# A graph network with layer norm on one core: transposes moved ahead of the next scores, mixing behind them, scores spread over three PSUM banks

## The chip, the cores and the metric

The kernel runs on one core of one Trainium2 chip. The metric is device time in microseconds (us) from launch to end; lower is better. Before the change it is 384.06 us, the median of three runs (383.94 to 384.15).

## The reference, cut to what matters

128 graphs of 64 nodes, 384 features each, and a 64 x 64 matrix of edge types (0 or 1 in this data) for each graph:

```
hi = h @ W1[:384] + emb[adj] @ W1[384:] + b1
hj = h @ W2[:384] + emb[adj] @ W2[384:] + b2
relevance[i, j] = sum over features of hi[i, j] * hj[i, j]
A    = softmax over j of where(adj != 0, relevance, -1e9)
h2   = relu((A @ h) @ gcn_w + gcn_b) @ Wo + bo
out  = layernorm(x + h2)
```

## The kernel before, in words

The weights are folded at the start, so that for two nodes joined by an edge the relevance is a bilinear form of x: a projection of x by one 384 x 384 matrix M, and a product with x. A group is 512 rows: 8 graphs, held as four "pairs" of 128 rows. There are 16 groups (0 to 15); `run` emits bodies 0 and 1, a hardware loop of two bodies for groups 2 to 13, then bodies 14 and 15 (`LAST` is 15). Products of large matrices run in fp32r with each operand split in a high and a low part, so each is three matmuls (L422, L423, L424 for projection and value, L515, L516, L521 for the output). Scores, transposes and mixing are plain fp32; a plain fp32 matmul shows as two records, a transpose as one.

TensorE carries for each group these stages, by function:

- `proj` (L426): 27 matmuls of 512 columns, K-block by K-block into three banks; ScalarE copies each finished bank with a bias to `gt_sb` (`project_out`, L714), and counts `gt_ready`.
- `score_stage` (L439): 24 fp32 matmuls, 128 rows x 64 columns of array, in bank 0, one graph of a column half at a time with its three blocks of K in a row. It begins with a wait for all three `gt_sb` blocks.
- VectorE then masks (`rel`, L921, four instructions, then L925 and L927), ScalarE exponentiates (`weigh`, L773), VectorE divides (L939, L941: `weights`, semaphore `normed`).
- `value` (L450): 36 matmuls, four banks (1 to 4), x times gcn_w; VectorE copies each to `hg_sb` (L825).
- `turn` (L478): two 128-column transposes of `weights` into bank 0; ScalarE copies them to `at_sb` (L795).
- `mix` (L485): 48 fp32 matmuls on 64 x 64 tiles of the array, in banks 4 to 7; ScalarE applies relu twice for each of three blocks (`hidden`, L781 and L783, counted by `hshi`), and VectorE makes the low part (`low_half`, L912, counted by `hslo`).
- `out` (L575): 36 matmuls into banks 5, 6, 7 and 1; VectorE adds x (L834, counted by `added`), takes statistics (L839) and normalises (L856), with GpSimd computing the inverse deviation (L1116).

The order on TensorE is written by hand, and each engine runs its own list in order; semaphores tie them. In a steady body g TensorE issues: mix(g-1), scores(g), value(g+1), out(g-1), turn(g), proj(g+1). Body 0 has no mix and no out, and its scores follow the second half of value(0). The last body issues mix(14), scores(15), the second half of out(13), half of out(14), turn(15), out(14) pair 2, mix(15), out(14) pair 3, and `out_last` follows. ScalarE's body g is: hidden(g-1), weigh(g), the high part of x two groups on (L708), `row_terms` of the next group (L723, the per-row term that L921 needs, semaphore `srow_ready`), the copy of the transposes (L795), `project_out(g+1)`. In the last body ScalarE runs hidden(14), weigh(15), the copy, hidden(15). SyncE loads x, its transpose and the edge matrix two groups ahead and stores results; the transposed x waits for `score_mm`, and the edge matrix for `masked`.

The first product of out(14) carries a condition of its own (L588):

```
if static(g, LAST - 1) and q == 0:
    pe.wait_ge(hshi, C * LAST if c == 0 else C * g + c + 1)
```

With C = 3 that asks for all three high blocks of group 14 (45 counts) before its first matmul.

Of the kernel before, what the change touches and what calls it, by code (L numbers as in the profile page):

```python
# [46 lines left out]
P = 128  # L47
# [5 lines left out]
def gnn_layernorm_kernel(nc, x, x_t, adj, adj_t, edge, biases, w1_t, w2_t, gcn_w, wo_w, wo_b, out):  # L53
    HID, TOKENS = x_t.shape
    NODES = adj.shape[2]
# [23 lines left out]
    with ExitStack() as ctx:  # L79
# [86 lines left out]
        score = bank[0]  # L166
        M_BANK = bank[5:8]
# [251 lines left out]
        def _(pe):  # L419
# [19 lines left out]
            def score_stage(g, par):  # L439
                pe.wait_ge(gt_ready, C * (g + 1))  # L440
                for n in range(PAIRS):
                    for c in range(C):
                        for e in range(2):
                            q, h = HALVES * e + n // 2, n % 2
                            ts = slice(q * P + h * NODES, q * P + (h + 1) * NODES)
                            mm = pe.matmul(score[e * NODES:(e + 1) * NODES, n * NODES:(n + 1) * NODES],  # L446
                                           gt_sb[:, c, ts], xt_sb[:, par, c, ts], start=(c == 0), stop=(c == C - 1))
                mm.then_inc(score_mm, 1)

            def value(g, par, q):  # L450

                if static(g, 0):
                    if q == 0:
                        pe.wait_ge(xt0_lo, 1)
                    elif q == 2:
                        pe.wait_ge(xlo, 1)
                elif q == 0:
                    pe.wait_ge(xlo, g + 1)
                    if static(g, 1):
                        pe.wait_ge(hg_ready, PAIRS)  # L460
                    elif not static(g, 2):
                        pe.wait_ge(added, PAIRS * (g - 2))
                elif q == 3 and not static(g, 1):
                    pe.wait_ge(hshi, C * (g - 1))
                ts = slice(q * P, (q + 1) * P)
                for c in range(C):
                    if static(g, 0) and q == 0:
                        pe.wait_ge(gcn_lo_ready, C + c + 1)
                    mm = three(VALUE_BANK[q][:, 0:HW], xt_hi[:, par, c, ts], xt_lo[:, par, c, ts],
                               gcn_hi[:, c, :], gcn_lo[:, c, :], c == 0, c == C - 1)  # L470
                mm.then_inc(value_mm, 1)
# [6 lines left out]
            def turn(g):  # L478
                pe.wait_ge(normed, 2 * (g + 1))
                for v in range(HALVES):  # L480
                    mm = pe.transpose(score[:, v * P:(v + 1) * P],  # L481
                                      weights[:, 2 * v:2 * v + 2, :].rearrange("p h n -> p (h n)"), ident[:])
                mm.then_inc(turn_mm, 1)
# [91 lines left out]
            def out(g, qs):  # L575

                for q in qs:
                    if q == 0 and not static(g, LAST - 1):
                        pe.wait_ge(hslo, C * (g + 1))
                    if static(g, LAST - 2) and q == 2:  # L580
                        pe.wait_ge(hg_ready, PAIRS * LAST + 1)
# [29 lines left out]
            def body(g, par):  # L611
                if not static(g, 0):
                    mix(g - 1, 1 - par)
                score_stage(g, par)
# [10 lines left out]
                if static(g, 0):  # L625
                    pe.wait_ge(ident_ready, 1)
                else:
# [3 lines left out]
                turn(g)  # L631
# [67 lines left out]
        def _(act):  # L699
# [85 lines left out]

            def body(g, par):
                if not static(g, 0):
                    hidden(g - 1)
# [5 lines left out]
                act.wait_ge(turn_mm, g + 1)  # L794
                act.copy(at_sb[:], score[:, 0:MIX]).then_inc(at_ready, 1)  # L795
                if before(g, LAST):
                    project_out(g + 1, PROJ1_BANK if static(g, 0) else PROJ_BANK)
                else:
                    hidden(g)
# [22 lines left out]
        def _(dve):  # L822
# [92 lines left out]
            def body(g, par):  # L915
# [4 lines left out]
                for q in range(PAIRS):  # L920
                    a = dve.scalar_tensor_tensor(rel[:, q, :], score[:, q * NODES:(q + 1) * NODES],  # L921
# [291 lines left out]
```

## Time and profile before

| | us |
|---|---|
| median of three runs | 384.06 |
| the profiled execution's own time | 387.24 |
| its span, first to last instruction | 385.4 |
| TensorE matmul busy | 376.2 (98%) |
| VectorE busy | 214.7 (56%) |
| ScalarE busy | 170.9 (44%) |
| GpSimd busy | 150.2 (39%) |

Matmuls are pipelined and the ends of their records are modelled, so the length of a matmul record is not its share of the time: the distance from one start to the next is. A busy share of 98% says that there is always a matmul under way, not that the array is full. A weight load (PEld) that starts together with the matmul of the same line had nothing to hide behind.

### The profile page before, as it was taken

To read this page: it belongs to the slowest core of one execution; us is meant where nothing else is said; L and a number is where in the kernel's file an instruction comes from. 1 tells how busy PE (TensorE), PEld (TensorE's weight loads), DVE (VectorE), ACT (ScalarE), POOL (GpSimd) and SP (SyncE) were. 2 spreads that over 40 slices of the span, in tenths; PEclk is the share of its full clock that TensorE was granted. 3 is DMA by queue.
4 is the path that set the end of the run, shared out by engine and by line. 5 is a ranking of instruction groups with operands and counts; after the bars stand their busy time and mean duration, and the time that the engine had idled before them with its cause. 6 is when DMAs were issued, how large, how long until landed. Compare 5 with 4: busy or idle time off the path is not lost.

```text
span 385.4 us, 10043 instructions
## 1 busy us (share of the span) xinstructions
PE 376.2 (98%) x3977; PEld 343.7 (89%) x3977; DVE 214.7 (56%) x528; ACT 170.9 (44%) x389; POOL 150.2 (39%) x133
## 2 busy tenths in 40 slices
PE   8999999999999999999999999999999999999992
PEld 4689898998989899898989989898998989898991
DVE  1535166563637656363755636375564637555684
ACT  1533561626336162633617263361726346153563
POOL 0031635080723508072350807245080724517043
PEclk9999999999999999999999999999999999999998
DMA  7922021707143170715317071531707153260105
GB/s 224 317 102 82 17 83 26 236 0 205 57 140 120 18 241 0 207 51 140 119 26 233 0 212 46 145 113 27 231 0 218 41 151 107 34 229 6 38 21 189
DMA packets 34820, 42.89 MB, mean 111 GB/s; under 512 B 10096, under 2 KB 29040, under 8 KB 34800
## 3 DMA queue, kind: packets, MB, share of 16 engines
q1 hardware_dynamic: 34144, 41.92, 36.1%
q10 hardware_dynamic: 656, 0.70, 0.7%
q8 instruction: 13, 0.21, 0.2%
q14 instruction: 7, 0.06, 0.1%
HBM read 30.03 MB, written 12.58 MB: 111 GB/s over the span
## 4 chain that ended last, share of the span: by engine, by line
PE 97%; DVE 2%; issue 0%; POOL 0%; DVEq 0%
PE banks L422 18%; PE banks L424 17%; PE banks L423 17%; PE banks L515 9%; PE banks L521 9%; PE banks L516 9%; PE banks L501 6%; PE banks L446 6%; PE banks L548 2%; PE banks L529 1%; PE banks L481 1%; DVE stats L839 1%; DVE xt_sb L834 0%; PE banks L556 0%; PE banks L540 0%
## 5 line engine op out<-in xcount | busy, mean ns | idle before, releaser
L1105 POOL TENSOR_TENSOR x_sb<-x_sb,wob_sb 128x1536 f32<-128x1536 f32 x15 | 52.5, 3503 | 177.7 <-DVE weights L941 177.7
L422 PE MATMUL banks<-gcn_hi,xt_hi 128*128 128x386 f32 x192 | 66.7, 347 | 0.0
L424 PE MATMUL banks<-gcn_hi,xt_lo 128*128 128x386 f32 x192 | 65.0, 339 | 0.0
L423 PE MATMUL banks<-gcn_lo,xt_hi 128*128 128x386 f32 x192 | 65.0, 338 | 0.0
L714 ACT ACTIVATE gt_sb<-banks,r_sb 128x512 f32<-128x512 f32 x48 | 33.0, 687 | 71.0 <-PE banks L424 70.9
L921 DVE SCALAR_TENSOR_TENSOR rel<-banks,srow,adj_sb 128x64 f32<-128x64 f32 x64 | 13.7, 278 | 85.5 <-PE banks L446 84.1
L515 PE MATMUL banks<-wo_hi,hs_hi 128*128 128x384 f32 x180 | 61.0, 339 | 0.0
L516 PE MATMUL banks<-wo_lo,hs_hi 128*128 128x384 f32 x180 | 60.9, 339 | 0.0
L521 PE MATMUL banks<-wo_hi,hs_lo 128*128 128x384 f32 x180 | 60.6, 339 | 0.0
L422 PE MATMUL banks<-xt_hi,m_hi 128*128 128x512 f32 x144 | 57.5, 399 | 0.0
L424 PE MATMUL banks<-xt_hi,m_lo 128*128 128x512 f32 x144 | 56.8, 394 | 0.0
L423 PE MATMUL banks<-xt_lo,m_hi 128*128 128x512 f32 x144 | 56.4, 392 | 0.0
L1096 POOL TENSOR_TENSOR xt_lo<-xt_sb,xt_hi 128x1536 fp32r<-128x1536 f32 x15 | 52.6, 3507 | 5.1 <-ACT xt_hi L708 5.1
L834 DVE TENSOR_TENSOR y_sb<-banks,x_sb 128x384 f32<-128x384 f32 x60 | 33.3, 556 | 29.9 <-PE banks L521 29.9
L825 DVE COPY hg_sb<-banks 128x385 f32<-128x385 f32 x64 | 35.6, 556 | 22.9 <-PE banks L424 22.8
L781 ACT ACTIVATE hs_sb<-banks,bias_sb 128x512 f32<-128x512 f32 x48 | 33.3, 695 | 16.3 <-PE banks L501 16.3
L422 PEld LDWEIGHTS banks<-gcn_hi,xt_hi 128*128 128x128 f32 x192 | 36.2, 188 | 1.1
L423 PEld LDWEIGHTS banks<-gcn_lo,xt_hi 128*128 128x128 f32 x192 | 36.4, 190 | 0.0
L424 PEld LDWEIGHTS banks<-gcn_hi,xt_lo 128*128 128x128 f32 x192 | 36.3, 189 | 0.0
L795 ACT COPY at_sb<-banks 128x256 f32<-128x256 f32 x16 | 6.0, 373 | 66.9 <-PE banks L481 66.8
L839 DVE BATCH_NORM_STATS2 stats<-y_sb 128x6 f32<-128x384 f32 x60 | 33.6, 560 | 2.0
L515 PEld LDWEIGHTS banks<-wo_hi,hs_hi 128*128 128x128 f32 x180 | 33.8, 188 | 0.1
(89 smaller groups left out, 585.0 us busy)
## 6 DMA issues: line engine op xcount, KB each, us to landing
xt_sb<-in_x_t_dram SPq DMA_DIRECT2D x15, 768.0 KB, 4.6
x_sb<-in_x_dram SPq DMA_DIRECT2D x15, 768.0 KB, 5.4
out_dram<-y_sb SPq DMA_DIRECT2D x30, 384.0 KB, 5.8
adj_sb<-in_adj_dram SPq DMA_DIRECT2D x32, 64.0 KB, 2.3
xt_sb<-in_x_t_dram SPq DMA_DIRECT2D x2, 384.0 KB, 8.4
xt_sb<-in_x_dram SPq DMA_DIRECT2D x1, 768.0 KB, 6.2
out_dram<-xt_sb SPq DMA_DIRECT2D x4, 192.0 KB, 2.0
w1t_sb<-in_w_t_dram ACTq DMA_DIRECT2D x3, 192.0 KB, 6.3
```

The lines of the kernel that those rows point to most:

```text
L422: pe.matmul(acc, a_hi, b_hi, start=first, stop=False)
L423: pe.matmul(acc, a_hi, b_lo, start=False, stop=False)
L424: return pe.matmul(acc, a_lo, b_hi, start=False, stop=last)
L515: pe.matmul(acc, hs_home(g)[0][:, c, ts], wo_hi[:, c, :], start=(c == 0), stop=False)
L516: pe.matmul(acc, hs_home(g)[0][:, c, ts], wo_lo[:, c, :], start=False, stop=False)
L521: mm = pe.matmul(out_bank(g, q)[:, 0:HID], hs_home(g)[1][:, c, ts], wo_hi[:, c, :], start=False, stop=(c == C - 1))
L781: act.activation(by_graph(hs_sb[:, f, :]), mixed(f), ACT.Relu, bias=gb_sb[:, f:f + 1]).then_inc(hsr, 1)
L825: dve.tensor_copy(hg_sb[:, slot, q, :], VALUE_BANK[q][:, 0:HID + 1]).then_inc(hg_ready, 1)
L834: dve.tensor_tensor(y_home(g, slot)[:, q, :], out_bank(g, q)[:, 0:HID], x_home(g, slot)[:, q, :], ALU.add).then_inc(added, 1)
L839: dve.bn_stats(stats[:, q, :], y_home(g, slot)[:, q, :]).then_inc(statd, 1)
L1096: pool.tensor_tensor(xt_lo[:, slot], xt_sb[:, slot], f32(xt_hi[:, slot]), ALU.subtract).then_inc(xlo, 1)
L1105: pool.tensor_tensor(x_home(g, slot), x_home(g, slot), wob_sb[:].rearrange("p (o n) -> p o n", o=1).to_broadcast([P, PAIRS, HID]), ALU.add ...
```

## The change

Transposes leave their place between out and proj. In a body g above 0 TensorE now begins with turn(g-1), then scores(g), then mix(g-1), then value(g+1), out(g-1), proj(g+1). The transposes write bank 5. The scores of graph n = 0, 1, 2 go to banks 0, 1, 2 and those of n = 3 to bank 0; for the first three graphs the first two blocks of K are done ahead of the third, and the wait for the third block of `gt_sb` stands between. Since banks 1 and 2 are also value's, value's first matmul waits for the masks of the body's scores to be read (`masked`), and so does out(13) pair 2 in the last body. The scores wait for all additions of out(g-2), and the transposes for bank 5 to be free. On ScalarE the copy of the transposes stands at the top of the next body, ahead of `hidden`. The wait for the identity matrix moves with the first transposes. Group 15's own transposes stay where they were.

```
+        SCORE_BANK = bank[0], bank[1], bank[2], bank[0]
+        TURN_BANK = bank[5]
...
             def score_stage(g, par):
-                pe.wait_ge(gt_ready, C * (g + 1))
-                for n in range(PAIRS):
-                    for c in range(C):
+                def graphs(n, blocks):
+
+                    for c in blocks:
                         for e in range(2):
                             q, h = HALVES * e + n // 2, n % 2
                             ts = slice(q * P + h * NODES, q * P + (h + 1) * NODES)
-                            mm = pe.matmul(score[e * NODES:(e + 1) * NODES, n * NODES:(n + 1) * NODES],
+                            mm = pe.matmul(SCORE_BANK[n][e * NODES:(e + 1) * NODES, n * NODES:(n + 1) * NODES],
                                            gt_sb[:, c, ts], xt_sb[:, par, c, ts], start=(c == 0), stop=(c == C - 1))
-                mm.then_inc(score_mm, 1)
+                    return mm
+
+                if static(g, LAST):
+                    pe.wait_ge(added, PAIRS * (g - 2))
+                elif not (static(g, 0) or static(g, 1)):
+                    pe.wait_ge(added, PAIRS * (g - 1))
+                pe.wait_ge(gt_ready, C * g + 2)
+                for n in range(PAIRS - 1):
+                    graphs(n, (0, 1))
+                pe.wait_ge(gt_ready, C * (g + 1))
+                for n in range(PAIRS - 1):
+                    graphs(n, (2,))
+                graphs(PAIRS - 1, range(C)).then_inc(score_mm, 1)
 
             def value(g, par, q):
...
                 elif q == 0:
+                    pe.wait_ge(masked, 3 * g - 2)
                     pe.wait_ge(xlo, g + 1)
...
             def turn(g):
                 pe.wait_ge(normed, 2 * (g + 1))
+                if static(g, 0):
+                    pe.wait_ge(gt_ready, C + 1)
+                elif static(g, LAST):
+                    pe.wait_ge(hshi, C * g)
+                else:
+                    pe.wait_ge(added, PAIRS * (g - 1) + 1)
                 for v in range(HALVES):
-                    mm = pe.transpose(score[:, v * P:(v + 1) * P],
+                    mm = pe.transpose(TURN_BANK[:, v * P:(v + 1) * P],
...
                     if static(g, LAST - 2) and q == 2:
+                        pe.wait_ge(masked, 3 * LAST + 1)
                         pe.wait_ge(hg_ready, PAIRS * LAST + 1)
...
             def body(g, par):
+                if static(g, 1):
+                    pe.wait_ge(ident_ready, 1)
+                if not static(g, 0):
+                    turn(g - 1)
+                score_stage(g, par)
                 if not static(g, 0):
                     mix(g - 1, 1 - par)
-                score_stage(g, par)
...
-                if static(g, 0):
-                    pe.wait_ge(ident_ready, 1)
-                else:
+                if not static(g, 0):
                     if static(g, 1):
                         pe.wait_ge(wo_lo_ready, 1)
                     out(g - 1, range(2 if static(g, LAST - 1) else PAIRS))
-                turn(g)
                 proj(g + 1, 1 - par, PROJ1_BANK if static(g, 0) else PROJ_BANK)
...
+            def turned_out(g):
+
+                act.wait_ge(turn_mm, g + 1)
+                act.copy(at_sb[:], TURN_BANK[:, 0:MIX]).then_inc(at_ready, 1)
+
             def body(g, par):
                 if not static(g, 0):
+                    turned_out(g - 1)
                     hidden(g - 1)
                 weigh(g)
...
-                act.wait_ge(turn_mm, g + 1)
-                act.copy(at_sb[:], score[:, 0:MIX]).then_inc(at_ready, 1)
                 if before(g, LAST):
                     project_out(g + 1, PROJ1_BANK if static(g, 0) else PROJ_BANK)
                 else:
+                    turned_out(g)
                     hidden(g)
...
-                    a = dve.scalar_tensor_tensor(rel[:, q, :], score[:, q * NODES:(q + 1) * NODES],
+                    a = dve.scalar_tensor_tensor(rel[:, q, :], SCORE_BANK[q][:, q * NODES:(q + 1) * NODES],
```

## Rows read from the trace of the kernel before

**Rows 1.** The page: busy time by engine, and the chain that ended last.

```profile
PE 376.2 (98%) x3977; PEld 343.7 (89%) x3977; DVE 214.7 (56%) x528; ACT 170.9 (44%) x389; POOL 150.2 (39%) x133
PE 97%; DVE 2%; issue 0%; POOL 0%; DVEq 0%
```

**Rows 2.** Waits: engine, tile, line, waited for; total us, times, longest us.

```profile
PE banks L529 <- DVE attn L860: 1.3, 1, 1.3
...
PEld banks L501 <- issue: 5.7, 16, 0.4
...
POOL x_sb L1105 <- DVE weights L941: 177.7, 15, 14.0
```

**Rows 3.** Timeline, steady body, around the transposes: start, us, engine, line, operation.

```profile
173.56 0.34 PE L521 MATMUL banks<-wo_hi,hs_lo 128*128 128x384 f32 x1
173.56 0.31 PEld L481 LDWEIGHTS banks<-ident,weights 128*128 128x128 f32 x2
173.74 0.38 PE L481 MATMUL banks<-ident,weights 128*128 128x128 f32 x2
173.84 0.19 PEld L422 LDWEIGHTS banks<-xt_hi,m_hi 128*128 128x128 f32 x1
...
174.19 0.39 PE L423 MATMUL banks<-xt_lo,m_hi 128*128 128x512 f32 x1
174.41 0.40 PE L424 MATMUL banks<-xt_hi,m_lo 128*128 128x512 f32 x1
```

**Rows 4.** Timeline, same body, TensorE from projection over mixing and scores to value.

```profile
179.92 0.40 PE L424 MATMUL banks<-xt_hi,m_lo 128*128 128x512 f32 x1
180.24 1.49 PEld L501 LDWEIGHTS banks<-at_sb,hg_sb 64*64 64x64 f32 x96 [0.36 <-issue]
...
181.80 1.48 PEld L446 LDWEIGHTS banks<-xt_sb,gt_sb 128*64 128x64 f32 x48
...
183.35 0.19 PEld L422 LDWEIGHTS banks<-gcn_hi,xt_hi 128*128 128x128 f32 x1
...
183.63 0.34 PE L423 MATMUL banks<-gcn_lo,xt_hi 128*128 128x386 f32 x1
```

**Rows 5.** Timeline, same body, ScalarE and VectorE.

```profile
174.15 0.37 ACT L795 COPY at_sb<-banks 128x256 f32<-128x256 f32 x1 [4.76 <-PE banks L481]
...
180.35 0.69 ACT L714 ACTIVATE gt_sb<-banks,r_sb 128x512 f32<-128x512 f32 x1 [1.38 <-PE banks L424]
...
181.94 0.69 ACT L781 ACTIVATE hs_sb<-banks,bias_sb 128x512 f32<-128x512 f32 x1 [0.90 <-PE banks L501]
...
183.47 0.86 DVE L921 SCALAR_TENSOR_TENSOR rel<-banks,srow,adj_sb 128x64 f32<-128x64 f32 x4 [5.55 <-PE banks L446]
```

**Rows 6.** Timeline, last body: VectorE's end of a block, and TensorE's release by it.

```profile
373.27 0.69 DVE L912 TENSOR_TENSOR hs_lo<-hs_sb,hs_hi 128x512 fp32r<-128x512 f32 x1
...
374.02 0.30 PEld L521 LDWEIGHTS banks<-wo_hi,hs_lo 128*128 128x128 f32 x2 [0.15 <-DVE hs_lo L912]
```

**Rows 7.** Timeline, body 0: scores, row terms, first value matmul, masks.

```profile
31.17 1.48 PEld L446 LDWEIGHTS banks<-xt_sb,gt_sb 128*64 128x64 f32 x48 [0.24 <-issue]
...
31.87 1.21 ACT L723 ACTIVATE srow<-hg_sb,k_sb 64x2 f32<-64x2 f32 x4 [3.08 <-DVE hg_sb L825]
32.72 0.45 PE L422 MATMUL banks<-gcn_hi,xt_hi 128*128 128x386 f32 x1
...
33.22 0.86 DVE L921 SCALAR_TENSOR_TENSOR rel<-banks,srow,adj_sb 128x64 f32<-128x64 f32 x4 [1.39 <-ACT srow L723]
```

**Rows 8.** Timeline, last body: hidden(14) on ScalarE, out(13) and out(14) on TensorE.

```profile
358.18 0.69 ACT L781 ACTIVATE hs_sb<-banks,bias_sb 128x512 f32<-128x512 f32 x1 [0.90 <-PE banks L501]
...
359.59 0.44 PE L515 MATMUL banks<-wo_hi,hs_hi 128*128 128x384 f32 x1
...
361.04 0.72 ACT L783 ACTIVATE xt_hi<-banks,bias_sb 128x512 fp32r<-128x512 f32 x1
...
362.87 0.33 PE L515 MATMUL banks<-wo_hi,xt_hi 128*128 128x384 f32 x1
```

## The prediction

> **What bounds the kernel now.** I read the page first. TensorE is busy 98% of the span and is 97% of the chain that ended last [rows 1], so an edit moves the time only if it lengthens or shortens TensorE's own sequence. The list of waits comes next: TensorE's longest is 1.3 us, at the very start, and no steady stage waits for another engine. What is left are small holes that the list calls "issue", 5.7 us over the 16 mixing stages, 0.36 each [rows 2]. Then the timeline of one steady body, read by distances between starts. In the projection a 512-column matmul starts 0.22 to 0.23 after the one before it (174.19 to 174.41) [rows 3]; an output matmul takes 0.18, since the transposes start 0.18 after the last of them (173.56 to 173.74) [rows 3], more exactly 0.176 (18 of them from 359.59 + 0.10 to 362.87) [rows 8]; value's, two columns longer, take the same.
>
> So the present cost of the transposes is: they start at 173.74, and the projection's second matmul at 174.19, of which 0.23 are its first one. 174.19 - 0.23 - 173.74 = 0.22 us per group. The mixing stage begins 0.32 after the start of the last projection matmul, which streams for 0.23: a hole of 0.09. Mixing takes 1.56 (180.24 to 181.80), the scores 1.55 (181.80 to 183.35), and value's first weights are loaded in the open: its second matmul starts 0.28 after the load instead of 0.18, 0.10 lost [rows 4].
>
> **The change, part by part.** Let S be the start of the last projection matmul (179.92 in the steady body), and all times below counted from it.
>
> *Transposes.* Leaving their place gives 0.22. In the new place the first follows the projection at 0.23, with its weights loaded behind it as they are behind the output matmul now [rows 3]. The second comes 0.10 later (its successor's load starts 0.10 after 173.74), at about 0.33, and streams some 0.05. Then comes a stage on another shape of tile. If it opens with the same hole as mixing does now (0.09 to 0.10), the scores' first load is at 0.49; mixing's was at 0.32. The two transposes cost 0.16 in the new place, and the move gains 0.22 - 0.16 = 0.06. The bounds: 0.03 (the hole is counted from the end of the longer fp32 record) and 0.15 (no hole at all after a transpose). Fifteen of the sixteen move (group 15's don't): 15 x 0.06 = -0.9 us, from -0.5 to -2.3.
>
> *The order of mixing and scores.* Both are small fp32 matmuls on two shapes of tile. Before, three changes of shape per body (projection to mixing, mixing to scores, scores to value); after, three again. I put the swap at 0.
>
> Why the hole should stay: mixing and scores are both fp32, and still the value stage shows its exposed load and mixing its hole at a change of shape [rows 4], while the output matmuls (fp32r, full array) pass to the transposes (fp32, full array) with none [rows 3]. The Trainium skill, "TensorEngine Tiling (Array Packing)", section Tiling Modes, says that a change of tiling mode, unlike a change of tile, drains the engine; by that rule the hole follows the shape of the tile and not the data type. It speaks against the hope that gathering the fp32 stages removes a transition, and the count of three before and three after stays; without it the sum would be lower by 15 x 0.09.
>
> *The wait for the third block of K.* ScalarE's copy of the third projection bank starts at 0.43 and takes 0.69 [rows 5]: ready at 1.12. TensorE sees a release about 0.06 later (VectorE ends at 373.96, the load goes at 374.02) [rows 6]: 1.18. The stage has 12 of its 24 matmuls to do before, 12 x 0.06 = 0.7 from 0.49: the load of the 13th is due at about 1.18. Before, mixing hid this copy; now it is met to the hundredth. I take 0 to 0.03 per group and carry +0.2 us over 15; the bound above is 0.1 each, +1.5, if the queue, empty by then, is slow to fill. In body 0 value's second half lies between, so nothing.
>
> *The wait for the copied transposes.* ScalarE takes it after the projection copy, at about 1.12, 0.37 long [rows 5]: ready by 1.55. Mixing is due at 0.49 + 1.55 = 2.04. Hidden behind the scores; without them it would cost 1.2 per group.
>
> *The new wait of value for the masks.* In a steady body VectorE begins L921 0.12 after the scores end (183.47 against 183.35) and needs 0.86 [rows 5], having been idle 5.55 before. From 2.04: masks read at 3.0, seen at 3.1; mixing lasts until 3.60. Hidden, with 0.5 to spare. Queued behind this wait are value, out and proj, everything, so where the cover is missing it is paid in full. It is missing in **body 0**, which has no mixing. There value starts at 32.72, but L921 starts only at 33.22, held by the row terms on ScalarE (31.87 + 1.21), and ends at 34.08 [rows 7]; released at 34.13. TensorE stands from 32.72 to 34.13: **+1.4 us**, and nothing after it has slack to absorb this.
>
> *Mixing 1.7 us later: what waits for it.* ScalarE's hidden starts 0.14 after mixing ends, so at 3.74 instead of 2.02 [rows 4, 5]. It takes 3.58 (358.18 to 361.76) [rows 8]: done at 7.32. In a steady body its first users are value's fourth bank, at 3.60 + 0.10 + 27 x 0.176 = 8.45, and out, at 10.1 with the low parts done by 8.1. Both hidden. GpSimd starts after the softmax, later by under 1.8, and waits 14 us at most for it, 177.7 in 15 waits [rows 2]. The loads of the transposed x and of the edges are issued earlier, since scores and masks are; SyncE has no new wait. In the **last body** the cover is thin: between mixing and out(14) lie only 18 matmuls. Before, hidden(14) ended at 361.76 and out(14) started at 362.87 [rows 8]. After: out(13) from 3.60 + 0.10 lasts 18 x 0.176 = 3.17, so the first load of out(14) is due at 6.70; it asks for all of hidden(14), seen at 7.38, and its load is then in the open. The matmul starts at 7.48 instead of 6.88: **+0.6 us** (0.4 to 0.8, as ScalarE's copies stretch). Pair 2 of out(13) waits for the masks as value does, and finds them read at 3.1. Group 15's softmax follows hidden(14) and is done about 9.3, its transposes are due at 10.6: covered. From there to the end the order is as before.
>
> **Sum.** -0.9 + 0.2 + 1.4 + 0.6 = +1.3 us; without the 0.2, +1.1. The profiled execution took 387.24 (span 385.4, 1.8 around it), 3.2 more than the median of 384.06, so a difference read from it is scaled by 0.99, which changes nothing. I predict **385.3 us**, own range 384.6 to 386.0.
>
> **The rivals.**
> 1. *The holes cost less or the move gains more, and the two stalls are cancelled.* If the transposes leave no hole the gain is 2.3 instead of 0.9: 384.06 - 2.3 + 2.0 = 383.8, within 0.2% of before (0.77 us, about what a measurement can tell). For: nothing shows a transpose ahead of a small tile. Against: rows 4.
> 2. *TensorE's supply fails between the small matmuls.* The stage of 24 scores now has a stop in it, and behind it follow mixing's several waits, with small matmuls that start every 0.016 us (96 in 1.56) [rows 4]. Now these waits are passed under long matmuls. If each of the two places (13th score, value after mixing) shows 0.05 to 0.1, 15 bodies add 1.5 to 3: 386.6 to 388.2. It decides if the stop lasts beyond 1.18 or the gap ahead of mixing grows over 0.1. For: the queue is empty at the stop. Against: before, one wait stood between mixing and scores, and the stretch is 1.56 like mixing alone.
> 3. *Faster.* The scores in three banks run quicker: today each of 24 matmuls takes 0.06; if those that now follow a matmul on another bank (9 of 24) took half, 9 x 0.03 x 16 = 4.3 us go, 381.0; it decides from 2 us on, if the scores stage falls below 1.42. For: each accumulates on what was just written. Against: mixing accumulates nothing and has the same pace per tile (96 records on four tiles, 48 on two, both in 1.56).
> 4. *The change doesn't do what it says.* If the masks' wait in body 0 were met early, 1.4 would go: 383.9. The rows leave no room for it; it is in rival 1's chance.
>
> **How the numbers follow.** Forecast 0.52, rival 1 0.20, rival 2 0.18, rival 3 0.10. The forecast's own range goes a little below 384.83 (slower by 0.2%), which moves 0.07 of it to the middle. Faster 0.10, same 0.26, slower 0.64. The range leaves out rival 3 and the upper half of rival 2: 383.7 to 387.0.
>
> **What would show it.** The list of waits has a new TensorE wait of 1.4 for L921's masks, once, and one of 0.6 at L515 for L783, once. L481 starts 0.23 after the last L424; the projection follows the output with no gap; the scores' first load is about 0.49 after the last L424; no gap within the scores; value's first load 3.6 after S. The distance from body to body falls by 0.06. Wrong would be: no wait in body 0, a steady body shorter by more than 0.15, or longer.

## The result, and the profile after

| | kernel before | kernel after |
|---|---|---|
| device time, median (lowest to highest), us | 384.11 (383.94 to 386.32), 4 runs | 390.22 (388.3 to 391.05), 4 runs |
| ratio to before, 95% interval | | 1.0127 (1.0093 to 1.0161) |
| span of the profiled execution, us | 385.4 | 388.2 |
| first score matmul to last matmul, us | 346.49 | 350.65 |

The ratio says that the change costs 1.3%, about 4.9 us (3.6 to 6.2); the two medians alone lie 6.1 apart, and I go by the ratio with its interval. 385.3 was forecast, with 387.0 as the upper end. The sign was right; the size was not.

The last line of the table is a measure that I use from here on: the distance between the starts of TensorE's first score matmul and of its last matmul, read from the trace. The whole span is a poor ruler, because the start-up varies by itself: the first scores began anywhere between 27.3 and 31.2 us in fourteen profiled executions, whatever the kernel. Behind them the work repeats to 0.01 us: three more profiled executions with the old order gave 346.48, 346.48 and 346.49.

The page of the kernel after, busy time and chain. TensorE still is the bound [rows 1], but "issue" (time in which the engine waited for nothing that the profile shows) has come into the chain with 1%, and so has ScalarE:

```profile
PE 375.1 (97%) x3977; PEld 344.5 (89%) x3977; DVE 218.1 (56%) x528; ACT 168.5 (43%) x389; POOL 150.2 (39%) x133
PE 94%; ACT 1%; DVE 1%; POOL 1%; issue 1%; DVEq 0%
```

The list of waits of the kernel after, TensorE's new entries (engine, tile, line, waited for; total us, times, longest us); it stands against [rows 2]:

```profile
PEld banks L448 <- issue: 2.8, 16, 0.2
...
PEld banks L522 <- issue: 2.4, 2, 2.1
...
PE banks L522 <- issue: 2.0, 1, 2.0
...
PE banks L424 <- DVE rel L949: 1.4, 1, 1.4
...
PEld banks L536 <- ACT xt_hi L806: 0.6, 1, 0.6
...
PE banks L536 <- ACT xt_hi L806: 0.3, 1, 0.3
```

PEld is the weight load and PE the matmul of the same stop, so two rows can tell of one. Three stops were forecast: 16 small holes, now ahead of the scores (L448) in place of mixing; once 1.4 us for the masks (VectorE's L949); and once 0.6 for hidden(14) (ScalarE's L806; 0.3 in the matmul's row). One was not: TensorE stood 2.0 us within the mixing stage (L522), once, and waited for no semaphore.

**A steady body.** Timeline of the kernel after, from the last projection matmul to mixing (start, us, engine, line, operation; in brackets the idle time before it and what ended it), against [rows 3, 4]:

```profile
157.18 0.39 PE L426 MATMUL banks<-xt_hi,m_lo 128*128 128x512 f32 x1
...
157.41 0.38 PE L502 MATMUL banks<-ident,weights 128*128 128x128 f32 x2
157.61 0.69 ACT L737 ACTIVATE gt_sb<-banks,r_sb 128x512 f32<-128x512 f32 x1 [1.37 <-PE banks L426]
157.72 1.48 PEld L448 LDWEIGHTS banks<-xt_sb,gt_sb 128*64 128x64 f32 x48 [0.17 <-issue]
...
158.20 0.36 ACT L812 COPY at_sb<-banks 128x256 f32<-128x256 f32 x1
159.27 0.27 PEld L522 LDWEIGHTS banks<-at_sb,hg_sb 64*64 64x64 f32 x12
```

The transposes start 0.23 after the last projection matmul, the scores' first load 0.31 later, at 0.54. The 48 score records run without a stop (1.55 to mixing's first load), although ScalarE's copy of the third block ends only at 158.30: the stage's second half, which needs it, is due at 158.5, so that wait is hidden, and so is the one for the copied transposes (158.56 against 159.27). A body takes 22.407 us, against 22.427 before: it gains 0.02.

**Body 0.** Timeline of the kernel after, VectorE's masks and value's first matmul, against [rows 7]:

```profile
30.80 0.46 PE L448 MATMUL banks<-xt_sb,gt_sb 128*64 128x64 f32 x10
31.70 0.86 DVE L949 SCALAR_TENSOR_TENSOR rel<-banks,srow,adj_sb 128x64 f32<-128x64 f32 x4 [1.39 <-ACT srow L746]
32.62 0.44 PE L424 MATMUL banks<-gcn_hi,xt_hi 128*128 128x386 f32 x1 [1.35 <-DVE rel L949]
```

The masks are read at 32.56 and TensorE goes on at 32.62, 0.06 later, as forecast.

**Body 14, the first one behind the loop.** Timeline of the kernel after:

```profile
338.80 1.21 PE L522 MATMUL banks<-at_sb,hg_sb 64*64 64x64 f32 x66
...
342.00 0.32 PEld L522 LDWEIGHTS banks<-at_sb,hg_sb 64*64 64x64 f32 x14 [2.12 <-issue]
342.00 0.46 PE L522 MATMUL banks<-at_sb,hg_sb 64*64 64x64 f32 x14 [1.99 <-issue]
342.38 0.19 PEld L424 LDWEIGHTS banks<-gcn_hi,xt_hi 128*128 128x128 f32 x1
```

82 of mixing's 96 matmuls are done, then nothing for 2 us, then the last 14. No engine's instruction releases them. The DMA view shows what happens there. The page of either kernel has a queue called "instruction" (q8) with 13 transfers in all; asked by windows, the first one behind the loop went at another moment. The kernel before, between 335 and 336 us (queue, kind: packets, MB, share of 16 engines):

```profile
q8 instruction: 1, 0.02, 7.2%
```

The kernel after, between 339.5 and 341 us; from 334 to 339.5 there is no such row:

```profile
q8 instruction: 1, 0.02, 3.7%
```

In the trace's record of transfers each is 16384 bytes. Before, it starts at 335.22, while TensorE still works through long projection matmuls, and mixing and scores follow at 337.2 to 340.3 without a gap. After, it starts at 339.57 and takes 0.88, to 340.45. TensorE's last matmul ahead of the pause starts at 339.80, the next one at 342.00, 1.55 behind the end of the transfer. That suggests that TensorE waited for its own code; the experiments below test it.

**The last body.** Timeline of the kernel after, against [rows 8]:

```profile
364.61 0.71 ACT L806 ACTIVATE xt_hi<-banks,bias_sb 128x512 fp32r<-128x512 f32 x1
364.72 0.33 PE L542 MATMUL banks<-wo_hi,hs_lo 128*128 128x384 f32 x1
365.38 0.45 PE L536 MATMUL banks<-wo_hi,xt_hi 128*128 128x384 f32 x1 [0.33 <-ACT xt_hi L806]
365.66 0.34 PE L537 MATMUL banks<-wo_lo,xt_hi 128*128 128x384 f32 x1
```

Matmul to matmul 0.66 instead of 0.18, and 0.28 instead of 0.18 to the one behind it, whose load is in the open: 0.6 for the 36 output matmuls (7.02 from the first to the transposes, against 6.40).

**The ledger**, from scores to scores, so that mixing, which changed its side, is counted alike (us):

| stretch | before | after | difference |
|---|---|---|---|
| scores(0) to scores(1), mixing(0) taken off before | 16.07 - 1.56 = 14.51 | 16.04 | +1.53 |
| scores(1) to scores(14), 13 bodies | 13 x 22.427 = 291.55 | 13 x 22.407 = 291.29 | -0.26 |
| scores(14) to scores(15) | 19.25 | 21.53 | +2.28 |
| scores(15) to the last matmul, mixing(14) added before | 19.61 + 1.56 = 21.17 | 21.80 | +0.63 |
| sum | | | +4.18, measured 350.65 - 346.49 = 4.16 |

So half of the loss is a thing that the prediction did not know. What may make up the rest of the 4.9 us came to light in the experiments, in the next section.

### The profile page after: what moved, and what is told of

Its sections match the earlier page's. It is cut to its first block, busy times and chain, and to the rows that moved or that the text cites. A ratio compares the mean times of both kernels' runs of the same rounds, so it can differ in the third digit from the quotient of the medians.

```text
span 388.2 us, 10086 instructions
## 1 busy us (share of the span) xinstructions
PE 375.1 (97%) x3977; PEld 344.5 (89%) x3977; DVE 218.1 (56%) x528; ACT 168.5 (43%) x389; POOL 150.2 (39%) x133
## 4 chain that ended last, share of the span: by engine, by line
PE 94%; ACT 1%; DVE 1%; POOL 1%; issue 1%; DVEq 0%
PE banks L424 18%; PE banks L425 17%; PE banks L426 17%; PE banks L536 8%; PE banks L537 8%; PE banks L542 8%; PE banks L522 7%; PE banks L448 6%; PE banks L569 2%; PE banks L550 1%; PE banks L502 1%; POOL rstd L1144 1%; ACT hs_sb L804 0%; PE banks L577 0%; ACT xt_hi L806 0%
## 5 line engine op out<-in xcount | busy, mean ns | idle before, releaser
L424 PE MATMUL banks<-xt_hi,m_hi 128*128 128x512 f32 x144 | 56.6, 393 | 0.0
L949 DVE SCALAR_TENSOR_TENSOR rel<-banks,srow,adj_sb 128x64 f32<-128x64 f32 x64 | 13.8, 277 | 61.6 <-PE banks L448 60.2
L542 PEld LDWEIGHTS banks<-wo_hi,hs_lo 128*128 128x128 f32 x180 | 33.6, 188 | 0.3
```

The costliest lines, as they stand in the source:

```text
L424: pe.matmul(acc, a_hi, b_hi, start=first, stop=False)
L542: mm = pe.matmul(out_bank(g, q)[:, 0:HID], hs_home(g)[1][:, c, ts], wo_hi[:, c, :], start=False, stop=(c == C - 1))
```

## The experiments

Each kernel was timed beside the kernel before on its chip. The kernel before had a median of 386.28 us in the first group of four, 385.69 in the second and 384.36 in the third.

**1. The kernel before once more.**

> The kernel before, unchanged. The profiled execution of it lasted 387.24 us and the median of its runs 384.06, 3.2 less; the changed kernel's profile opens with the second matmul stage (L569) 1.5 us shorter than before's (L548), because the full clock was granted 3 us earlier. If the gap of 3.2 lies in the start-up clock, a second profile of this kernel shows a span near 383.8 with L548 at 7.5 us instead of 9.0, or again 385.4 with 9.0. If there is something else that comes and goes, the spans differ while L548 is the same, and a pause on TensorE or a late load must show in one of them and not in the other.

One execution: 385.15 us, span 383.3. First scores at 28.70 instead of 31.17, and from there to the last matmul 346.48, the same as in its first profile. The 2.1 us that the span is shorter come from the start (2.5 less, and 0.3 more behind the last matmul). The windows of the first profile, from 0, 8 and 13.5 us (us, busy and instructions of PE, PEld, DVE, ACT, POOL, granted clock, DMA share, GB/s):

```profile
8.00:13.50 5.50, 5.50 (x10) 2.92 (x9) 1.64 (x3) 2.06 (x4) 0.00 (x0) 1.00 1.10 333
```

and of this execution:

```profile
8.00:13.50 5.50, 4.92 (x20) 3.01 (x19) 1.19 (x2) 1.60 (x3) 0.00 (x0) 1.00 1.07 335
```

TensorE did ten matmuls of the set-up in one and twenty in the other. This has nothing to do with the change; it is why differences are read from the first scores on. The expectation's first branch holds in the main: the stage of 18 set-up matmuls (L548) took 9.0 us in the first profile and 6.9 in this one. The trace's record of the granted clock begins, at full speed, at 13.3 us in the first and at 4.2 in this one; the 1.00 in the rows above says nothing for the time before, of which there is no record. All fourteen profiles fit this: in seven the full clock is on record from 4.2 to 6.0 us on, and the first scores start at 27.3 to 28.7; in six it is from 10.2 to 13.3 on, and they start at 29.1 to 31.2. The last one (number 7) has it from 4.4 on, but half clock again from 14.7 to 18.1, and starts at 29.7.

**2. No masked wait in body 0.** Scores(0) in one bank in the old order, and no wait ahead of value(1).

```diff
+                if static(g, 0):
+                    pe.wait_ge(gt_ready, C)
+                    for n in range(PAIRS):
+                        last = graphs(n, range(C), bank[0])
...
-                    pe.wait_ge(masked, 3 * g - 2)
+                    if not static(g, 1):
+                        pe.wait_ge(masked, 3 * g - 2)
```

> The changed kernel with the scores of group 0 alone kept in bank 0 and in the old order, so that value of group 1 needn't wait for the masks. Theory (stalls add up): TensorE's wait of 1.4 us for L949 is gone and nothing takes its place; the time is 1.4 us below the changed kernel, about 388.8, and the 2 us pause in mixing of body 14 stays. Rival (slack later absorbs it): less than 0.5 us is gained, and another wait of TensorE grows. The scores of group 0 being in one bank could also show whether three banks matter: their stage of 48 records should last the same 1.55 us.

Ratio 1.0106 (1.005 to 1.0161). Scores(0) to scores(1) fell from 16.04 to 14.61: the wait was worth 1.43, and it is gone. The whole time did not reach the 388.8 that was expected (389.98, and the interval is too wide to tell 1.4 us). The profiled execution lost some 1.5 us elsewhere. Its windows around the pause, columns as above:

```profile
338.40:341.40 3.00, 1.01 (x26) 0.81 (x18) 0.54 (x2) 0.33 (x1) 0.00 (x0) 0.99 0.98 359
341.40:344.80 3.40, 3.40 (x12) 3.40 (x12) 0.85 (x2) 3.40 (x8) 0.00 (x0) 0.51 0.11 36
344.80:350.00 5.20, 5.20 (x32) 5.20 (x31) 3.60 (x8) 1.43 (x9) 2.60 (x1) 1.00 0.00 0
```

In the first window TensorE stands for 2 us. In the second it is busy throughout, at a granted clock of 0.51, that is 1.2 GHz instead of 2.4, and starts 12 matmuls in 3.4 us; at full clock it would be some 19. Scores(14) to scores(15) took 23.07, against 21.53 in the first profile of the kernel after: 1.54 more. The pause can bring a second loss with it.

**3. The load of x(15) held back.** The DMA engines are full when the code block is fetched (share 1.03 from 337 to 340 us in the kernel after), and this load (the issue at 338.63 in the kernel after) is part of it.

```diff
+                        sp.wait_ge(mix_mm, LAST - 1)
```

> The changed kernel with one more wait on SyncE: the load of x for group 15, which now leaves at 338.63, 1.4 us into the dense matmuls of body 14, waits for mixing(13) to end. Theory A (the pause of 2.2 us in that mixing is TensorE waiting for its next 16 KB block of instructions, whose transfer at 339.7 to 340.6 stands in line behind data transfers, since all 16 DMA engines are busy from 337 on): the block comes earlier and the pause falls to under 1 us or goes; time about 388.2 to 389. Theory B (the block is asked for only when the sequencer runs into its edge, and takes 2.3 us whatever else is moving): the pause stays at 2.0 to 2.3 us and the time is that of the changed kernel, 390.

Ratio 1.0149 (1.0082 to 1.0216). The load left at 343.16, behind the pause. The pause stayed, behind the same 82nd matmul, and was 0.3 longer. Timeline of TensorE:

```profile
338.87 1.49 PE L523 MATMUL banks<-at_sb,hg_sb 64*64 64x64 f32 x82
342.62 0.45 PE L523 MATMUL banks<-at_sb,hg_sb 64*64 64x64 f32 x14 [2.26 <-issue]
```

The load of x(15) is not the cause. How much of the 2 us other transfers add was not settled; in no run were the DMA engines free at the pause (share 0.97 ahead of it here and 0.55 during it).

**4. The code shifted by 84 instructions.** Increments of a semaphore of which nobody's wait depends, spread over TensorE's bodies 0 and 1 ahead of the loop. Nothing in the order of the work changes; the code behind them stands 84 places further on.

```diff
+                for _ in range(min(2, padding[0])):
+                    pe.sem_inc(mix_begun, 1)
+                    padding[0] -= 1
...
+            padding[0] = 84
```

> The changed kernel with 84 semaphore increments that nobody waits for among TensorE's instructions of bodies 0 and 1, two ahead of every three long matmuls, where the sequencer has time. They move everything behind them by 84 places against the 256-instruction blocks in which code is fetched. Theory B (where a block ends decides): the pause in body 14 moves from the 82nd mixing record to some 42 records earlier, or goes to another stage, or is gone where the edge falls under long matmuls. Theory A (load traffic alone): the pause stays at about 340 us and at the same record, give or take. The increments themselves should cost nothing; if they do, it is seen as a longer distance from body 0 to body 2.

Ratio 1.0032 (0.9998 to 1.0065), 1.2 us over before instead of 4.9. No pause: scores(14) to scores(15) 19.23. A block was fetched at 102.4, inside the first turn of the loop, where before and after fetch none past 96.9. First scores to last matmul 348.55, 2.06 over before. The wait in body 0 grew by 0.24 (1.81 from start to start instead of 1.58) in all padded versions of the new order that have it. That is the padding's own doing: two of the idle increments stand between the wait and value's first matmul, and the trace has them at 30.64 and 30.79, behind the masks, and the matmul at 30.90.

**5. The kernel before shifted by 24**, to make it pay the pause.

```diff
+                for _ in range(min(1, padding[0])):
...
+            padding[0] = 24
```

> The kernel before with 24 idle semaphore increments in body 0's value and projection, and nothing else. Theory B (the pause belongs to where the code blocks end against the loop's exit, not to the new order): the old order now has a pause of some 2.2 us too, in the first 300 records of body 14, between 337 and 341 less the start-up difference, and the distance from the scores of group 1 to the last matmul grows from 330.4 to about 332.6. Rival (the new order's own waits starve TensorE): no pause, 330.4. The increments are hidden either way.

A miss: ratio 0.9986 (0.996 to 1.0011), no pause, a block fetched inside the loop (104.4), 346.48 from the first scores to the last matmul.

**6. The kernel after with 8 instructions fewer** (one warm-up matmul instead of three).

```diff
-WARM_UP = 3
+WARM_UP = 1
```

> The changed kernel with one warm-up matmul instead of three, which takes 8 instructions out ahead of the loop. By the places of the pauses seen so far the block edge lies some 13 instructions behind the loop's exit in the changed kernel and 16 in the one before; if so small a margin decides, 8 fewer bring the fetch back to the exit and the pause in mixing of body 14 is gone, as in the kernel before. If the pause stays, the margin is another, or the order matters too. The clock may come up at another time, so the distance from the scores of group 1 to the last matmul is what counts: 334.6 with the pause, 332.4 without.

A miss as well: ratio 1.0149 (1.0093 to 1.0204). The pause stayed (2.16 from start to start), and the half clock followed it.

**7. Shifted by 84, and the condition in front of out(14) relaxed**: its first block asks only for the first of the three parts of hidden(14).

```diff
-                            pe.wait_ge(hshi, C * LAST if c == 0 else C * g + c + 1)
+                            pe.wait_ge(hshi, C * g + c + 1)
```

> The changed kernel with the 84 increments and with the first matmul of out(14) asking for the first high block of group 14 alone (hshi 43) instead of all three. Theory (the tail's stall is the condition's): the gap of 0.66 from start to start at the first matmul of out(14) falls back to 0.18, no other gap takes its place, and the distance from the scores of group 1 to the last matmul is 0.48 less than with the increments alone. Rival (the chain is held by ScalarE's hidden all the same): a gap of 0.2 to 0.6 appears at the second or third block, or at the transposes of group 15, and under 0.2 is gained.

Ratio 1.006 (1.0024 to 1.0096); first scores to last matmul 348.23, 0.32 less than number 4. The gap of 0.66 has gone, and the three blocks of out(14)'s first pair run without a stop. One of 0.36 has come ahead of its second pair, with 0.10 behind it for a load that has nothing to hide behind. Timeline:

```profile
363.38 0.69 DVE L950 TENSOR_TENSOR xt_lo<-hs_sb,xt_hi 128x512 fp32r<-128x512 f32 x1 [0.46 <-ACT xt_hi L816]
...
364.00 0.55 DVE L872 TENSOR_TENSOR y_sb<-banks,x_sb 128x384 f32<-128x384 f32 x1
...
364.60 0.19 PEld L545 LDWEIGHTS banks<-wo_hi,xt_hi 128*128 128x128 f32 x1 [0.28 <-DVE y_sb L872]
```

The second pair waits for VectorE's addition of out(13)'s third pair (`added`). In VectorE's list that addition stands behind the low parts of all three blocks of group 14 (L950), and the last of these waits for ScalarE's hidden(14). So what is left is another wait than the condition's, passed on from the late hidden(14) by VectorE.

**8. All three costs taken away**: numbers 2, 4 and 7 together.

> The changed kernel with all three repairs: scores of group 0 in one bank without value's wait, the 84 increments, and the shorter condition on out(14). If the steady state is worth what the traces show (22.405 against 22.427 per body, 0.02 x 12 = 0.3 us) and the three stalls are all that the change cost, this one is the same as the kernel before within 0.3 us, on the fast side, and no gap between matmuls is above 0.33 us. If something else was lost, it is slower than before by more than 1 us and the gaps show where.

Ratio 1.0007 (0.9976 to 1.0037), 346.62 from the first scores to the last matmul, against 346.49 before. With the three losses repaired the new order is worth what the old one was; it is not on the fast side of it, as was expected, since the gap of 0.36 in the last body is there as in number 7. No version of the new order was faster than before.

**9. Shifted by 24.** The two misses showed that I didn't know where the edge between two code blocks lies, so I counted: with a load and a matmul for each record, the loop of the kernel after ends at TensorE's instruction 1987 and the pause stands at 2259, 272 behind it. The count is good to some six: in the trace 132 matmuls, as many loads and two waits lie between, 266. The Trainium skill, "Runtime: NRT & Kernel Launch", section Instruction fetch mechanics, has blocks of 16 KiB, 256 instructions; by that figure of the Trainium skill another edge lies, as an estimate, some 10 to 16 instructions behind the exit. The size of a block agrees with the transfers of 16384 bytes.

```diff
+            padding[0] = 24
```

> After with 24 idle increments of a semaphore on TensorE in bodies 0 and 1. Counting two instructions (load and matmul) for each matmul record, TensorE's loop ends at its instruction 1987 in after and the pause stood at about 2259; with 16 KB blocks of 256 instructions the edge of a block then lies at about 2003, 16 instructions behind the loop's exit. 24 more instructions bring that edge 8 instructions ahead of the exit. Theory (it decides on which side of the exit the edge stands): a block is fetched inside the loop, near 103 us, and mixing(13) shows no pause; scores to scores of bodies 14 and 15 is 19.2 us, the first scores to the last matmul as in the run with 84 increments, 332.3 less some 0.1; about 2.2 us less than the changed kernel run beside it. Rival (a long shift is needed, or the place in the mixing stage matters): the pause of 2.2 us is there, 24 instructions earlier in the code.

Ratio 1.0046 (1.0019 to 1.0073). No pause, 348.54; fetched inside the loop, in the window 104 to 106:

```profile
q8 instruction: 1, 0.02, 3.3%
```

**10. Shifted by 8 only.**

```diff
+            padding[0] = 8
```

> After with 8 idle increments. The edge of the block is then still behind the exit, by some 8 instructions. Theory: no fetch inside the loop after 97 us, pause of 2.2 us in mixing(13) 4 matmuls earlier (78 instead of 82 matmuls into the stage). Rival: no pause, the block fetched at the exit as in the kernel before; then some instructions decide and not the side of the exit.

The miss that tells most: one execution, 385.87 us, and no pause, 348.54 from the first scores to the last matmul. Nothing is fetched inside the loop after 94.7; the block comes at its exit, between 332 and 333 us, as in the kernel before:

```profile
q8 instruction: 1, 0.02, 5.5%
```

and the stage that held the pause runs through. Timeline of TensorE:

```profile
334.96 0.38 PE L512 MATMUL banks<-ident,weights 128*128 128x128 f32 x2
335.27 1.62 PE L457 MATMUL banks<-xt_sb,gt_sb 128*64 128x64 f32 x48
336.82 1.63 PE L532 MATMUL banks<-at_sb,hg_sb 64*64 64x64 f32 x96
338.38 0.44 PE L424 MATMUL banks<-gcn_hi,xt_hi 128*128 128x386 f32 x1
```

**11. The kernel before with 8 fewer**, the counterpart of number 6.

```diff
-WARM_UP = 3
+WARM_UP = 1
```

> The kernel before with one warm-up matmul instead of three, 8 instructions fewer. In before the block is fetched at 335.2, while TensorE still works on projection(14), with the edge 15 instructions behind the exit; here it is 23 behind. Theory 1 (the new order of stages makes the late fetch): fetched near the exit as before, no pause, 19.25 us from scores to scores of bodies 14 and 15. Theory 2 (the code's place alone makes it, the old order pays it too): the fetch comes on demand within the scores of body 14, some 80 matmuls of mixing and scores later, and TensorE stands 2.2 us there: 21.5 us from scores to scores or within them.

Theory 1's numbers: ratio 1.0003 (0.9973 to 1.0032), fetched at 333.2, no pause, 346.49.

**12. The kernel after once more.**

> The changed kernel once more, beside the padded one. Theory: gaps of 1.58, 2.2 and 0.66 us in the same places as in its first profile, 334.6 us from the scores of group 1 to the last matmul; 2.2 us and at times another 1.6 (half clock behind the pause) more than after with 24 increments. Rival (the pause was an accident of single executions): absent here.

389.81 us (387.66 to 392.6), ratio 1.0126 (1.008 to 1.0173), the first result again. The pause is in its place and a little longer, and this time the half clock follows. Its windows:

```profile
337.00:340.00 3.00, 1.16 (x76) 1.02 (x66) 1.49 (x6) 0.00 (x0) 0.00 (x0) 1.00 1.06 386
340.00:343.50 3.50, 3.08 (x22) 2.97 (x23) 0.00 (x0) 2.33 (x5) 0.00 (x0) 0.51 0.34 126
343.50:350.00 6.50, 6.50 (x39) 6.50 (x38) 4.37 (x9) 3.16 (x14) 2.52 (x1) 1.00 0.00 0
```

First scores to last matmul 352.25, 1.60 over the first profile of the same kernel: 0.27 for the longer pause and 1.3 for the half clock.

All versions by that measure:

| kernel | shift | last block of the loop, or first behind it, fetched at | pause | half clock behind it | first scores to last matmul |
|---|---|---|---|---|---|
| before, before again, before with one warm-up | 0, 0, -8 | 335.2, 332.8, 333.2 | no | no | 346.49, 346.48, 346.49 |
| before | +24 | 104.4 (in the loop) | no | no | 346.48 |
| after | 0 | 339.6 | 2.20 | no | 350.65 |
| after, again | 0 | 338.1 | 2.48 | yes | 352.25 |
| after | -8 | 339.6 | 2.16 | yes | 352.03 |
| after, x(15) held back | 0 | 340.2 | 2.48 | no | 350.93 |
| after, no wait in body 0 | 0 | 338.3 | 2.20 | yes | 350.75 |
| after | +8 | 332.0 | no | no | 348.54 |
| after | +24 | 104.9 (in the loop) | no | no | 348.54 |
| after | +84 | 102.4 (in the loop) | no | no | 348.55 |
| after, condition relaxed (number 7) | +84 | 102.9 (in the loop) | no | no | 348.23 |
| after, all three (number 8) | +84 | 98.7 (in the loop) | no | no | 346.62 |

The pause is measured from start to start, the times of fetches are from the trace's record of transfers on the instruction queue. In all five profiles with a pause TensorE goes on 1.4 to 1.6 us behind the end of the late transfer.

## Why the prediction was wrong in size, point by point

**Right: the wait in body 0.** +1.4 forecast. The list of waits has 1.4 for the masks, the ledger 1.53 for the stretch, and taking it away gave 1.43. The release of 0.06 after VectorE's end held.

**Right: the last body.** 0.6 forecast for hidden(14), 0.63 in the ledger, 0.62 of it in the output stage. Relaxing the condition gave back 0.32, so about half is the condition's alone. The other half stays lost with the condition relaxed, at a wait that the forecast did not name: VectorE's addition for out(14)'s second pair, itself held by hidden(14) (number 7).

**Right: the hidden waits.** The third block of K, the copied transposes and value's wait in steady bodies show no gap. The forecast carried +0.2 for the first of these; it cost nothing. The sum had put half of the scores stage at 12 x 0.06 = 0.7, where half of 1.55 is 0.78, and so saw no slack; the third block is ready 0.2 ahead of its use (158.30 against 158.5).

**Mis-sized: the transposes.** The step "the scores' first load is at 0.49" was wrong by 0.05: the load is at 0.54, since it follows the second transpose's start by 0.20 (0.54 - 0.34) and not by 0.16 (0.49 - 0.33). The two transposes cost 0.21 in the new place (0.54 - 0.33) and 0.23 in the old; the body is 0.02 shorter and not 0.06, and 15 of them are worth 0.3 instead of 0.9. The hole at a change of tile shape stayed, as the Trainium skill's "TensorEngine Tiling (Array Packing)", section Tiling Modes, would have it, and behind the transposes it is larger (0.15, with the forecast's 0.05 for the second one's stream) than the 0.09 behind the projection [rows 4]. With this and the 0.2 put right, the forecast's own terms would have given 1.4 + 0.6 - 0.3 = +1.7 instead of +1.3; the ledger without the pause has +1.9.

**Wrong: the sum left out TensorE's code.** The failed step is the sum itself, "-0.9 + 0.2 + 1.4 + 0.6 = +1.3 us". Its four terms are all holes and waits; it took every stage whose waits are met to run at its pace, and so put the supply of TensorE's code at nothing without a reason. It did so everywhere except in one place, behind the loop's exit, where TensorE stood 2.2 us, as far as the runs show for a block of code. Rival 2 was the nearest to it: TensorE's supply failing between small matmuls. It named the symptom and the place in the order of stages, but had it as 0.05 to 0.1 in each of 15 bodies. What came is one pause of 2.2 to 2.5, in one body, inside mixing and not at its start; the steady bodies show none.

What is shown of its cause: the pause goes with a late fetch (five profiles of five), and goes away with 8, 24 or 84 idle instructions ahead of the loop (three of three, and two more with other edits), at -2.11 net of the 0.2 that the padding adds in body 0, so 2.3. It is no property of the new order of transposes, scores and mixing as such: the same order runs without it. Where the transfer starts under the projection's matmuls, 0.23 each (2.0 us ahead of mixing in the kernel before, 2.9 ahead of the transposes with a shift of 8), nothing is lost; in the kernel after it starts in the midst of matmuls that start every 0.016, 0.2 us before they stop.

The same section of the Trainium skill's "Runtime: NRT & Kernel Launch" says that the engine fetches the next block while it executes the current one and that the cost of an edge is mostly hidden. The runs agree with this: in the bodies no other transfer of the thirteen shows a gap in either kernel. That section of the Trainium skill also says that a taken branch with a far target forces a fetch. The runs do not show that: the loop's branch was taken at 108.6, 153.4, 198.2, 243.0 and 287.9 us in the kernel after, each time back to the loop's start, and nothing was fetched between 96.9 and 339.6. The one transfer that cost something is the first behind the turn in which the branch was not taken, and here it cost 2.2 to 2.5 us.

What stays open: why the fetch at the loop's exit goes out early with 8 more instructions and late with none or 8 fewer, while the old order has it early with none and 8 fewer (with 24 more either order fetches inside the loop). The count of instructions to the edge (16 in the kernel after, 15 in the kernel before, each good to some six) does not tell these apart, so something else than the side of the exit decides, and number 10, of which there is one execution, refuted the theory under which it ran. The traces have one thing more, TensorE's own branch and waits. In three profiles of the old order, unshifted or 8 fewer, the transfer starts 2.1 us behind the loop's last branch, and with +8 in the new order 1.1 behind it. In the five late ones it starts 6.9 to 7.3 behind it. Between lies a wait that only the new order has: that of the scores for the additions (L456), which the kernel after passes at 335.53, 2.9 behind the branch. It may be this wait that holds the fetch back; no run tested it. In that the change is not wholly innocent; by how much its order and by how much its place in the code, no run separated.

**The rest of the 4.9.** 4.16 is what the first profile of the kernel after shows. In three of the five profiles with a pause the granted clock fell to 1.2 GHz right behind it for 3.4 us, and cost 1.3 to 1.6 more. Three fifths of 1.5 is 0.9; 4.16 + 0.9 = 5.1, against 4.9 measured with an interval of 3.6 to 6.2. This is an estimate from five profiles; what each timed run lost is not on record. The prediction had no such term.

**Rival 3** (scores in three banks run quicker) falls: the stage takes 1.55 as before. **Rival 1** would have needed holes that cost less; they cost more. **Rival 4** falls too: the masks' wait in body 0 was there, with 1.4.

## What to carry to other kernels

Before an edit in a tuned, nearly gapless kernel is judged by its time, look for pauses that wait for nothing, and ask the DMA view for the instruction queue around them. An edit changes the place of all code behind it, and here 8 idle instructions were worth 2.1 us in the one profile that has them (24 and 84 the same), more than everything that the edit meant to do: a kernel should be timed with a few shifts of its code before an order of stages is called slower. A wait that is added for all groups, or work that is moved later in all, costs where its cover is missing, here in the first and the last body, and that can be read from the trace before; it was right here to 0.1 us.

## What the runs showed of the hardware that was not expected

- One fetch of a 16384-byte code block in the open stops TensorE for 2.2 to 2.5 us, though the transfer itself takes 0.88; TensorE goes on 1.4 to 1.6 us behind its end, in five profiles of five. No other transfer in the bodies shows a gap.
- After such a pause of 2.2 us the granted clock fell to half for 3.4 us in three profiles of five, and cost another 1.3 to 1.6 us.
- Behind an fp32 transpose the first load of a smaller tile starts 0.20 after the transpose's start, where 0.16 had been expected.
- From the first scores to the last matmul executions of the old order repeat to 0.01 us, and so do the three shifted versions of the new one, while the start ahead of it varies by up to 4 us, and goes with the moment from which the full clock is on record (4.2 to 13.3 us).
